# First attention in split fp32r: V and the turned probabilities as high and low parts, with the low parts made by VectorE behind each row maximum

## What is computed

```
q = (x @ Wq + bq).reshape(Bsz, Tlen, NUM_HEADS, HEAD_DIM)
k, v = split(x @ Wkv + bkv)
q, k = q + pe, k + pe
scores = where(causal, (q @ k^T) / sqrt(128), min)
probs = softmax(scores)
out = (probs @ v).reshape(Bsz, Tlen, NUM_HEADS * HEAD_DIM)
return out @ Wo
```

## Time and profile before

| | |
|---|---|
| median of 3 runs | 759.58 us (756.88 to 760.53) |
| profiled execution | 764.21 us, its span 762.4 us |
| busy share of the span: TensorE, VectorE, ScalarE, GpSimd | 88%, 71%, 54%, 31% |
| first attention, from its first scores to its last projection | about 42 to 233 us |
| mean granted TensorE clock | 0.951 |

### The profile page before, as it was taken

How to read it: one execution, slowest core, us unless ns; L and a number is a source line. 1 busy time by engine, 2 the same in 40 slices (tenths; PEclk the granted TensorE clock), 3 DMA queues, 4 the chain that set the end, 5 groups by cost and what they waited for, 6 DMA issues and landing times. The chain is left out here.

```text
span 762.4 us, 11200 instructions
## 1 busy us (share of the span) xinstructions
PE 672.0 (88%) x3434; PEld 467.7 (61%) x3446; DVE 539.8 (71%) x830; ACT 410.7 (54%) x825; POOL 236.7 (31%) x183
## 2 busy tenths in 40 slices
PE   3988999999998989888899999998679779888685
PEld 2856777677765984544566566565535779878332
DVE  6165444344422224439899999999999999999998
ACT  1145665555651545575766667665746556666220
POOL 0012202212200005100222432332012866788874
PEclk9999999999997899999999999999969899999688
DMA  8400000000055482012366867778782454554112
GB/s 294 156 4 12 8 8 7 14 10 8 8 170 166 140 294 56 18 36 89 91 149 165 202 177 195 180 176 211 196 212 72 139 171 125 160 162 119 31 44 81
DMA packets 59806, 86.79 MB, mean 114 GB/s; under 512 B 7505, under 2 KB 35922, under 8 KB 59762
## 3 DMA queue, kind: packets, MB, share of 16 engines
q1 hardware_dynamic: 41330, 57.89, 24.6%
q0 software_dynamic: 7680, 23.08, 14.1%
q10 hardware_dynamic: 10752, 5.24, 2.3%
HBM read 54.60 MB, written 14.81 MB: 91 GB/s over the span
## 5 line engine op out<-in xcount | busy, mean ns | idle before, releaser
L1578 DVE TENSOR_REDUCE nmax<-PS 128x1 f32<-128x128 f32 (+7 forms) x128 | 96.1, 751 | 109.0 <-PE PS L1015 108.7
L1043 PE MATMUL PS<-ROOM 128*128 128x512 f32 (+3 forms) x384 | 141.7, 488 | 0.7 <-ACT ROOM L682 0.7
L682 ACT COPY ROOM<-PS 128x512 f32<-128x512 f32 (+1 forms) x192 | 85.8, 483 | 91.9 <-PE PS L1027 91.0
L689 ACT ACTIVATE ROOM<-PS,nmax 128x128 f32<-128x128 f32 (+7 forms) x128 | 95.6, 747 | 47.7 <-DVE nmax L1578 45.6
L1027 PE MATMUL PS<-CST,ROOM 128*128 128x128 f32 x576 | 85.9, 277 | 7.0 <-ACT ROOM L682 7.0
L559 POOL DMA_DIRECT2D ROOM<-ROOM x32 | 28.4, 889 | 202.0 <-DVE ROOM L1662 202.0
L1027 PEld LDWEIGHTS PS<-CST,ROOM 128*128 128x128 f32 x576 | 64.6, 142 | 34.3 <-issue 24.5
L1043 PEld LDWEIGHTS PS<-ROOM 128*128 128x128 f32 x384 | 65.0, 191 | 29.8 <-issue 25.8
L1012 PE MATMUL PS<-LATER 128*128 128x512 f32 (+2 forms) x192 | 74.5, 498 | 7.0 <-ACT ROOM L689 3.9
L524 POOL DMA_INDIRECT rows_in<-XN,slot x48 | 66.6, 1388 | 27.7 <-DVE slot L1491 14.4
L1654 DVE TENSOR_TENSOR_SCAN ROOM<-ROOM 128x1024 f32<-128x1024 f32 x32 | 72.8, 2275 | 0.9 <-ACT ROOM L725 0.2
(11 more groups left out here) (178 smaller groups left out, 1238.3 us busy)
## 6 DMA issues: line engine op xcount, KB each, us to landing
ROOM<-bc_rows SPq DMA_DIRECT2D x32, 512.0 KB, 4.3
ROOM<-ROOM POOLq DMA_DIRECT2D x32, 512.0 KB, 6.2
LATER<-in_w SPq DMA_DIRECT2D x48, 256.0 KB, 2.8
ROOM<-in_w SPq DMA_DIRECT2D x32, 321.0 KB, 3.8
rows_in<-zero SPq DMA_DIRECT2D x20, 256.0 KB, 3.3
LATER<-rows_in SPq DMA_DIRECT2D x24, 128.0 KB, 2.5
rows_out<-ROOM ACTq DMA_DIRECT2D x24, 128.0 KB, 2.2
ROOM<-rows_in SPq DMA_DIRECT2D x8, 256.0 KB, 4.2
```

Source lines behind the costliest of these rows:

```text
L682: nc.scalar.copy(dst, src).then_inc(s_ed, 1)
L689: nc.scalar.activation(PR[:, s, 0:nk], sc[:, 0:nk], ACT.Exp, bias=nmax[:, i % 4:i % 4 + 1], accum_out=rsum[:, i:i + 1]).then_inc(s_ex, 1)
L1043: r = mm(PS[:, 6, lo:BANK], V[:, j, :], PT[:, 4 * group + j, lo:BANK], start=j == 0, stop=True, skip_group_check=True)
L1578: nc.vector.tensor_reduce(nmax[:, i % 4:i % 4 + 1], sc[:, 0:(i + 1) * P], AX_X, ALU.max, negate=True).then_inc(s_nm, 1)
```

## The change

V of batch 0 becomes VH (ScalarE's copy from PSUM, now with an fp32r result) and VL (PSUM minus VH, on VectorE). The turned probabilities become PTH (ScalarE's copy) and PTL (PSUM minus PTH, on VectorE, `turned_low`). Each f32 product of `out_part` in batch 0 becomes three fp32r products: VH with PTH, VH with PTL, VL with PTH. `turned_low` stands on VectorE directly behind `neg_max` of the step in which the turn takes place, ahead of what stood beside the step before. TensorE waits in batch 0 for the new low counts (`s_el`, `s_vl`) where it waited for ScalarE's (`s_ed`, `s_ve`), both before it reuses a transpose bank and before the products. The new tiles lie in memory that is in use only later. Batch 1 is as before. The core of the diff:

```diff
+        with ExitStack() as first_split:
+            PTH = split_tile("PTH", [P, 12, BANK])
+            PTL = split_tile("PTL", [P, 12, BANK])
+            VH, VL = (split_tile(n, [P, TB, D]) for n in ("VH", "VL"))
...
-                    nc.scalar.copy(V[:, 4 * (q % 2):4 * (q % 2) + 4, :], bank(VALUE_BANK[q])).then_inc(s_ve, 1)
+                    nc.scalar.copy((V if b else VH)[:, 4 * (q % 2):4 * (q % 2) + 4, :], bank(VALUE_BANK[q])).then_inc(s_ve, 1)
...
-                    dst, src = turned(PT, i, part, c)
+                    dst, src = turned(PTH if split else PT, i, part, c)
                     nc.scalar.copy(dst, src).then_inc(s_ed, 1)
...
-            pe.wait_ge(s_ve, 2)
+            pe.wait_ge(s_vl, 2)
...
-            def turn(g, i, first=False):
+            def turn(g, b, i, first=False):
+                left = s_ed if b else s_el
                 pe.wait_ge(s_ex, 8 * g + i + 1)
                 for part in range(1 if i < 4 else 2):
                     c = i if i < 4 else 4 + 2 * (i - 4) + part
                     if not (first and c < 2):
-                        pe.wait_ge(s_ed, 12 * g + c - 1)
+                        pe.wait_ge(left, 12 * g + c - 1)
...
             def out_part(g, b, group, part, free=True):
+                ready = s_ed if b else s_el
                 if part == 0:
-                    pe.wait_ge(s_ed, 12 * g + (11 if group else 4))
+                    pe.wait_ge(ready, 12 * g + (11 if group else 4))
...
                 for j in ((2 * part, 2 * part + 1) if group else (part,)):
                     lo = max(0, j - 4 * group) * P
-                    r = mm(PS[:, 6, lo:BANK], V[:, j, :], PT[:, 4 * group + j, lo:BANK], start=j == 0, stop=True,
-                           skip_group_check=True)
+                    if b:
+                        r = mm(PS[:, 6, lo:BANK], V[:, j, :], PT[:, 4 * group + j, lo:BANK], start=j == 0, stop=True,
+                               skip_group_check=True)
+                    else:
+                        r = three(PS[:, 6, lo:BANK], (VH, VL), (PTH, PTL), (slice(None), j, slice(None)),
+                                  (slice(None), 4 * group + j, slice(lo, BANK)), j == 0)
...
                     tt(KL[:, sl], QF, KH[:, sl].bitcast(F32), ALU.subtract).then_inc(s_ke, 1)
+                    dve.wait_ge(s_ve, q + 1)
+                    t4 = slice(4 * q, 4 * q + 4)
+                    tt(VL[:, t4, :], bank(VALUE_BANK[q]).rearrange("p (t d) -> p t d", d=D), VH[:, t4, :].bitcast(F32),
+                       ALU.subtract).then_inc(s_vl, 1)
...
+            def turned_low(g, i):
+                for part in range(1 if i < 4 else 2):
+                    c = i if i < 4 else 4 + 2 * (i - 4) + part
+                    dve.wait_ge(s_ed, 12 * g + c + 1)
+                    dst, src = turned(PTL, i, part, c)
+                    tt(dst, src, turned(PTH, i, part, c)[0].bitcast(F32), ALU.subtract).then_inc(s_el, 1)
...
                 for i in range(8):
                     neg_max(g, i)
+                    if i < 2 and pending and not batch[0]:
+                        turned_low(g - 1, 6 + i)
+                    if i >= 2 and not batch[0]:
+                        turned_low(g, i - 2)
                     if beside and i in beside:
                         beside[i]()
...
             def head_end(g):
+                if not batch[0]:
+                    turned_low(g, 6)
+                    turned_low(g, 7)
```

More of the change, by code:

```diff
@@ L136, in build, with split_tile @@
         HEAD_END, MOE_END, END = 53 * KB, 90 * KB, 133 * KB
+        with ExitStack() as first_split:
+            def split_tile(name, shape, dt=F32R):
+                return first_split.enter_context(nc.sbuf_tensor(name, shape, dt))
+            split_tile("under_PTH", [P, 29 * KB], F32)
+            PTH = split_tile("PTH", [P, 12, BANK])
+            split_tile("under_PTL", [P, MOE_END + 2 * KB - HEAD_END], F32)
+            PTL = split_tile("PTL", [P, 12, BANK])
+            VH, VL = (split_tile(n, [P, TB, D]) for n in ("VH", "VL"))
+            split_tile("under_KH", [P, END - MOE_END - 34 * KB], F32)
+            KH, KL, QH, QL = (split_tile(n, [P, T]) for n in ("KH", "KL", "QH", "QL"))
         ROOM = sb("ROOM", [P, END])
-        with ExitStack() as first_split:
-            KH, KL, QH, QL = (first_split.enter_context(nc.sbuf_tensor(n, [P, T], F32R)) for n in ("KH", "KL", "QH", "QL"))
         LATER = sb("LATER", [P, 4 * T])
@@ L235, in build @@
         s_ve = sem("values_ready")
+        s_vl = sem("values_low_ready")
         s_ein = sem("gate_exponent_in")
@@ L256, in build @@
         s_ed = sem("probsT_ready")
+        s_el = sem("probsT_low_ready")
         s_pv = sem("head_out_in_psum")
@@ L674, in query_out, with keep_turned @@
                                      ).then_inc(s_qr, 1)
-            def keep_turned(g, i):
+            def keep_turned(g, i, split=False):
                 for part in range(1 if i < 4 else 2):
@@ L707, in head @@
                     if i < 2 and pending:
-                        keep_turned(g - 1, 6 + i)
+                        keep_turned(g - 1, 6 + i, split)
                     if i >= 2:
-                        keep_turned(g, i - 2)
+                        keep_turned(g, i - 2, split)
                     exps(g, i)
@@ L732, in attention_first @@
                 head(7, True, False, True)
-                keep_turned(7, 6)
+                keep_turned(7, 6, True)
                 out_evac(0, 15)
-                keep_turned(7, 7)
+                keep_turned(7, 7, True)
                 out_evac(1, 16)
@@ L1039, in out_part @@
                 if part == 2 and group:
-                    pe.wait_ge(s_ed, 12 * g + 12)
+                    pe.wait_ge(ready, 12 * g + 12)
                 for j in ((2 * part, 2 * part + 1) if group else (part,)):
                     lo = max(0, j - 4 * group) * P
-                    r = mm(PS[:, 6, lo:BANK], V[:, j, :], PT[:, 4 * group + j, lo:BANK], start=j == 0, stop=True,
-                           skip_group_check=True)
+                    if b:
[4 more added lines that the diff above has]
+                                  (slice(None), 4 * group + j, slice(lo, BANK)), j == 0)
                 if part == 3:
@@ L1092, in head @@
                     if i < 2 and pending:
-                        turn(g - 1, 6 + i)
+                        turn(g - 1, b, 6 + i)
                     if i >= 2:
-                        turn(g, i - 2, isinstance(g, int) and g == 0)
+                        turn(g, b, i - 2, isinstance(g, int) and g == 0)
                     if i == 0 and pending:
@@ L1110, in head_end @@
             def head_end(g, b, h, between=None):
-                turn(g, 6)
+                turn(g, b, 6)
                 out_part(g, b, 0, 2)
                 out_part(g, b, 0, 3)
-                turn(g, 7)
+                turn(g, b, 7)
                 for part in range(4):
```

## The result

The changed kernel takes 765.63 us, the one before 758.88 us beside it on the same chip (medians of 16 runs each): 6.75 us more. The ratio of the two, formed from all runs, is 1.0101 with a 95% interval of 1.0074 to 1.0128 (the quotient of the two medians is 1.0089, which lies inside it). The forecast was 766.8 us in a range of 761.5 to 771.5. The total came out as foretold, and in part by luck: head 0 with its clock was forecast 2.2 us too dear, and the heads behind it 1.7 us too cheap, and these errors nearly cancel. The experiments are about those.

The account below looks back on a forecast made before the run. TensorE was taken to bound the attention, 22.8 us a head. Net +2.3 us behind head 0, +3.3 in head 0 and +0.6 at the end made +6.2; with 1 for the clock, +7 on 759.6: 766.8 us, range 761.5 to 771.5.

Parts of the forecast that it names:

- head 0: First head, bound by VectorE, which also routes tokens: low parts make the last maximum 2.5 us later; +3.3 us in all.
- the heads behind it: From head 1's scores to head 7's end: products gain 8.3 us, stalls cost 3.4, 3.6 and 3.6; net +2.3 us.
- TensorE's own work: Output products of each head: three fp32r products replace one f32, 6.55 us instead of 7.7, a gain of 1.15 us.
- The low parts: Twelve VectorE subtractions a head: 0.69, 0.56, 0.42 and 0.29 us for 512, 384, 256 and 128 columns, some 6.8 us together.
- B: Stall at i = 2: TensorE's turn(0) waits for the low part behind ScalarE's copy of turn(7)'s first half; 0.52 us.
- A: Stall at i = 0: TensorE's turn(6) waits for a low part behind VectorE's 1024-column maximum; 0.56 us.
- C: Stall at i = 6: low(3) delays query evacuation and cast, so project waits for ScalarE's output copy behind them; 0.6 us.
- The clock: Head 0: TensorE's idleness lowers its clock to 1.2 GHz for a while; 1 us added, with ends 0 and 3.7.
- Rival 4: Clock stays low in head 0 as long as the start's, or falls again later: +10 to +14, 770 to 774 us; chance 0.15.
- The end: Head 7: the closing products start 1.56 us late but take 4.66 instead of 5.6; +0.6 us.
- The later stages: Stages behind the attention: untouched, they only start earlier or later by what the attention gains or loses.
- The first: Rival: low parts hand over faster than read and the three stalls vanish; 755 us, or 753 with head 0's delay halved; chance 0.07.

Follow-up runs that it names:

- e1_products: Changed kernel without the low parts' subtractions, the second of three products taking the high part again; ratio 0.988 to the kernel before.
- e6_fill_bc: On top of e5_query_first, the first project of step 2 goes ahead of turn(0) on TensorE; 759.71 us beside 759.14 for the kernel before, one execution.
- e7_all_three: Changed kernel with output products ahead of turn(6), project ahead of turn(0), query evacuation ahead of the low parts; 755.63 us beside 759.14 for the kernel before.
- e2_waits: Changed kernel with one f32 product of the high parts instead of three; low parts made and waited for, but unused; ratio 1.0239 to the kernel before.
- e3_low_last: Changed kernel with the low parts at the end of each VectorE step, behind additions, query evacuation and routing; ratio 1.0124 to the kernel before.
- e5_query_first: Changed kernel with VectorE's query evacuation ahead of the low parts in steps 1 and 5; 762.14 us beside 759.14 for the kernel before, one execution.

## Why the prediction came out

**TensorE's own work: right.** 1.15 us a head forecast, 1.17 by e1_products. The narrow products gain nothing, as forecast: the step from 0 to 1, which has those of 256 and 128 columns, takes 1.89 with three products and 1.86 with f32. Those of 512 start 0.23 apart, against 0.86 for one f32 product. By the four passes of the Trainium skill ("FP8 and Floating Point Precision", section TensorE Precision Notes), with an fp32r product taken as one, the estimate was 1.9; the rows decided, and the runs agree with the rows.

**The low parts: right.** 0.69, 0.56, 0.42 and 0.29 us for 512, 384, 256 and 128 columns, each as forecast.

**The stalls: right in place and cause, B 0.14 us short in price.** Forecast were 0.56 for A, 0.52 for B and 0.6 for C; a step with a stall is longer than the same step in e1_products by 0.57, 0.66 and 0.63. The lateness itself was right: turn(6) and turn(0) start 0.52 late, and `project` starts 0.63 later after its mask than in e1_products (in the same head 1.54 and 0.91). For C nothing comes on top, and for A 0.05. For B it is 0.14, and that is what the sum missed, since it held only the time until the waiting instruction may start. Behind the stall at 116.61 the first product starts 0.19 later, where in e1_products it starts 0.04 behind turn(0) when nothing is waited for:

```profile
107.63 0.28 PE L1039 MATMUL PS<-CST,ROOM 128*128 128x128 f32 x1
107.67 0.48 PE L1008 MATMUL PS<-PTH,VH 128*128 128x512 f32 x1
107.99 0.39 PE L1009 MATMUL PS<-PTH,VH 128*128 128x512 f32 x1
```

Nineteen stalls at the measured prices are 6 x 0.57 + 7 x 0.66 + 6 x 0.63 = 11.8 us, against the 10.6 of the sum, and 1.0 of that difference is B. It is 1.2 of the 1.7 us by which the forecast (+2.3) missed +4.03. The gain was taken at 8.3 and is 8.05: between the same two masks e1_products takes 146.63 us, the kernel before 154.68. That is 0.25 more. The remaining 0.26 is what the changed kernel takes over e1_products beyond the nineteen stalls, in head 6 and head 7; it was not traced.

**Head 0: +3.3 forecast, +2.1 measured (0.2 of it a later start of the whole head); the step that failed is the 2.5 us by which the last maximum was to be later.** It starts at 62.84 instead of 61.60, 1.24 later. The low parts did come in the queue as forecast, but another instruction became shorter. VectorE and GpSimd of the kernel before:

```profile
59.07 1.27 POOL L538 TENSOR_TENSOR QL<-ROOM,QH 128x512 fp32r<-128x512 f32 x1 [9.26 <-ACT QH L668]
59.25 1.57 DVE L1499 TENSOR_TENSOR tl<-re,CST 128x448 f32<-128x448 f32 x1
```

and of the kernel after:

```profile
60.20 1.27 POOL L548 TENSOR_TENSOR QL<-ROOM,QH 128x512 fp32r<-128x512 f32 x1 [10.20 <-ACT QH L678]
61.44 0.61 DVE L1516 TENSOR_TENSOR tl<-re,CST 128x448 f32<-128x448 f32 x1
```

The routing's comparison takes 0.61 us by itself, and 1.57 when GpSimd's subtraction has begun 0.18 ahead of it. After the change it comes when that is ending: 0.96 us that I had counted as VectorE's work was a collision, and 2.5 - 0.96 leaves 1.5. The 0.3 from there to the 1.24 seen is low(1). It was priced at 0.36 and moved the next maximum by 0.03 (from 51.45), since VectorE had a gap in front of it:

```profile
51.48 0.82 DVE L1599 TENSOR_REDUCE nmax<-PS 128x1 f32<-128x640 f32 x1 [0.50 <-PE PS L1025]
```

I had used the row of the comparison without asking why 448 columns should cost more than twice the 0.69 of a subtraction of 512. From the maximum to the scores (66.24) are 3.40 us (forecast 3.35).

**The clock: the fall was right, its price was nothing in this execution.** The stretch of the kernel after (columns as in the first view, the granted clock third from the end), and its TensorE in it:

```profile
60.00:65.00 5.00, 3.34 (x15) 3.21 (x16) 4.76 (x10) 3.54 (x8) 1.27 (x1) 0.66 0.00 0
```

```profile
61.48 1.51 PE L1039 MATMUL PS<-CST,ROOM 128*128 128x128 f32 x6 [2.47 <-DVE PTL L1608]
62.64 0.67 PE L1008 MATMUL PS<-PTH,VH 128*128 128x384 f32 x1
63.11 0.52 PE L1009 MATMUL PS<-PTL,VH 128*128 128x384 f32 x1
63.43 0.52 PE L1010 MATMUL PS<-PTH,VL 128*128 128x384 f32 x1
...
64.80 0.96 PE L1039 MATMUL PS<-CST,ROOM 128*128 128x128 f32 x7 [0.18 <-DVE PTL L1608]
66.64 0.23 PE L1025 MATMUL PS<-causalb,identb 128*128 128x128 bf16 x1
```

Granted 0.66 from 60 to 65 us, after 2.47 us of idleness; six transposes take 1.51 us (0.82 to 0.83 at the higher level) and the products of 384 columns start 0.32 apart instead of 0.17. That is the 1.2 GHz level, and by 64.80 it is back at 2.4. But turn(6) could not have started before its low part, made from 63.97 to 64.66, was there. All the slow work lies under that wait, which is shortened to 0.18 us; it costs nothing that can be seen. I should have asked what hides a fall of the clock, as of every other cost: here the same wait that causes it. In e6_fill_bc the same stretch stayed at the lower level up to 66.00, past that wait, and cost 1.6 us, as shown above. So the 1 us of the sum lies between what two executions show, and one trace can't tell its mean. Rival 4 did not come about; the gaps of 0.5 us in later heads left the granted clock at 1.00.

**The end:** 0.8 instead of 0.6. The closing products begin 6.38 us after the last mask, where the sum had 6.21.

**The later stages** do not move by the same amount in a single execution, as the prediction wanted for its test; they vary by 7 us by themselves. That test was a poor one. In the medians the attention's difference (+6.9 at batch 1's keys, against 6.75) does arrive.

**The rivals.** The first (the stalls vanish) was wrong for the kernel as changed, and e7_all_three shows what it would have needed: not faster hand-overs but other work in front of the waiting instruction. C was not covered by ScalarE's slack, since ScalarE's queue is in program order and the cast heads it.

## What to carry to other kernels

When an engine that never waits gets an operand with one more producer, price the new stalls as the end of the producer's chain, with 0 to 0.15 us for the restart, not by the share of busy time: VectorE was half idle, and the three stalls still cost 1.9 us a head against a gain of 1.2. First look for what stands behind the waiting instruction and does not need the operand, and put it in front; three moves of a few lines took all the stalls of the middle heads away. At the end of head 7 the same move only passed the stall on to the next turn, so look for the wait behind the one that you fill. And where an instruction's duration in a row doesn't fit its size, find out why before it goes into a sum.

## What the hardware showed that was not expected

- **A wait can cost more than the waiting.** At B the step is 0.14 us longer than the 0.52 by which turn(0) was late, at A 0.05, at C nothing. At B it is seen between turn(0) and the first product: 0.19 us behind the stall, 0.04 without one. In e2_waits, where an f32 product follows, it is 0.20 behind the stall, and 0.12 in the kernel before without one. What the engine does in that time, and why C has none of it, no row shows.
- **A comparison on VectorE that shares its time with GpSimd.** The same instruction, 448 columns with both inputs in SBUF, takes 1.57 us in the kernel before and in e1_products, 0.98 in e3_low_last, and 0.61 to 0.62 in the others; it is long exactly where GpSimd's subtraction of 512 columns has begun ahead of it and still runs. In the rows of the kernel before, above, GpSimd's ends at 60.34, VectorE's at 60.82, 0.48 later, so most of VectorE's instruction was done after the other. In e5_query_first the collision falls on other instructions of the routing, and GpSimd is held up too:

```profile
54.78 0.56 DVE L1502 TENSOR_TENSOR rt<-tl,rt 128x224 f32<-128x224 f32 x1
54.81 1.70 POOL L548 TENSOR_TENSOR QL<-ROOM,QH 128x512 fp32r<-128x512 f32 x1 [7.46 <-ACT QH L678]
55.38 1.37 DVE L1503 TENSOR_TENSOR rt<-rt,re 128x224 f32<-128x224 f32 x1
```

  VectorE's first has begun ahead, and GpSimd's takes 1.70 us instead of 1.27; VectorE's second (0.39 in the kernel before) then takes 1.37 and ends 0.24 after GpSimd's. The Trainium skill, "SBUF — State Buffer", section "SBUF: two separate sides", says that a VectorE operation with two SBUF inputs and a GpSimd operation that reads SBUF share a port pair by an exclusive lock, held by whichever started first for its whole instruction. These rows agree, in both directions. The low parts, which have one operand in PSUM, show no such lengthening: 512 and 128 columns take 0.89 us together at 60.64 in the changed kernel, while GpSimd's subtraction runs from 60.20 to 61.47, which is their 0.69 and 0.29 less the overlap of some 0.08.
- **The granted clock and the speed of the products don't always go together.** From 40 to 45 us the record grants 1.00 in the kernel after, yet three products of 256 columns start 0.38 and 0.22 apart there (44.25, 44.63, 44.85) and 0.16 and 0.12 at 66.24, 66.40 and 66.52. I can't say which of the two records is at fault; where both are at hand, the spacing of equal products is the one to sum with.
